# Expert rows in blocks of 256 and of 128 rows, and another order of the work between the attention loop and the second expert layer

## The reference, cut to what matters

```python
xn = layernorm(x)
s = L0_attn(xn)            # 16 heads of 64, ALiBi, two null keys
g = silu(L0_ffn(xn))       # top 1 of 8 experts: gelu(x @ W1[e] + b1[e]) @ W2[e] + b2[e]
x = x + s * g
xn = layernorm(x)
s = L1_attn(xn)            # one head of 128, layer norm, output projection
g = silu(L1_ffn(xn))       # top 2 of 8 experts, capacity C = 2*2*T/8 rows for each
x = x + s * g
```

## Time and profile before

| | |
|---|---|
| median of three runs | 1130.6 us (1126.27 to 1135.07) |
| the profiled execution | 1132.19 us, its span 1130.3 us |
| mean granted TensorE clock | 0.951 |
| busy: TensorE matmul | 1004.9 us, 89% |
| busy: VectorE, ACT, GpSimd | 686.6, 655.2, 673.2 us (about 60% each) |
| DMA | 103.70 MB, mean 92 GB/s |
| chain that ended last | TensorE 62%, VectorE 17%, ACT 7% |

### The profile page before, as it was taken

How to read it: one execution, slowest core, us unless ns; L and a number is a source line. 1 busy time by engine, 2 the same in 40 slices (tenths; PEclk the granted TensorE clock), 3 DMA queues, 4 the chain that set the end, 5 groups by cost and what they waited for, 6 DMA issues and landing times.

```text
span 1130.3 us, 22358 instructions
## 1 busy us (share of the span) xinstructions
PE 1004.9 (89%) x6636; PEld 736.4 (65%) x6636; DVE 686.6 (61%) x2541; ACT 655.2 (58%) x1967; POOL 673.2 (60%) x825
## 2 busy tenths in 40 slices
PE   6688899999999999899999998998889979999940
PEld 2465566666668986566666665666568758989940
DVE  6847776776753346776786777868654443445326
ACT  4329767667754557667666766675554434454534
POOL 5534588888754555676675687887354423545533
PEclk9759899999999999999999999999999889999985
DMA  9200202202526742303302212132130044777755
GB/s 300 58 6 1 43 25 61 65 25 66 160 47 209 221 129 63 74 6 70 65 7 60 54 36 61 34 67 53 40 86 19 29 144 144 214 216 217 214 139 142
DMA packets 97385, 103.70 MB, mean 92 GB/s; under 512 B 10447, under 2 KB 85238, under 8 KB 97040
## 3 DMA queue, kind: packets, MB, share of 16 engines
q1 hardware_dynamic: 90256, 89.96, 30.5%
q0 software_dynamic: 7040, 12.66, 3.3%
HBM read 77.29 MB, written 25.28 MB: 91 GB/s over the span
## 4 chain that ended last, share of the span: by engine, by line
PE 62%; DVE 17%; ACT 7%; issue 6%; POOL 4%; DMA 1%; another core or an unknown queue 1%; SPq 0%; POOLq 0%; DVEq 0%; ACTq 0%
PE bank L1135 11%; PE bank L644 9%; PE bank L633 9%; PE bank L1164 7%; PE bank L1191 5%; PE bank L1179 4%; PE bank L1216 4%; DVE arena L1760 4%; PE bank L1154 3%; ACT arena L1494 3%; DVE arena L1769 2%; POOL arena L910 2%; PE bank L1365 2%; PE bank L1349 1%; ACT arena L1483 1%
## 5 line engine op out<-in xcount | busy, mean ns | idle before, releaser
L1494 ACT ACTIVATE arena<-arena 128x128 f32<-128x128 f32 (+1 forms) x512 | 226.9, 446 | 114.6 <-DVE arena L1760 114.0
L1760 DVE CUSTOM_DVE_ANT_0 arena<-bank,arena 128x128 f32<-128x128 f32 (+1 forms) x512 | 183.0, 413 | 140.8 <-PE bank L1164 133.1
L1135 PE MATMUL bank<-arena 128*128 128x512 f32 x384 | 215.6, 649 | 13.0 <-ACT arena L1483 10.0
L910 POOL TENSOR_TENSOR arena<-arena 128x512 f32<-128x512 f32 x128 | 133.5, 1046 | 146.6 <-ACT arena L1470 141.7
L1769 DVE COPY arena<-bank 128x384 f32<-128x384 f32 x256 | 130.2, 549 | 24.5 <-PE bank L1179 21.4
L607 POOL DMA_INDIRECT expert_out<-arena x78 | 77.0, 988 | 100.8 <-DVE arena L713 85.1
L1470 ACT ACTIVATE arena<-bank 128x512 f32<-128x512 f32 x192 | 112.4, 586 | 31.1 <-PE bank L1135 30.9
L925 POOL TENSOR_TENSOR arena<-arena 128x512 f32<-128x512 f32 x128 | 129.5, 1045 | 1.3
L1164 PE MATMUL bank<-arena 64*128 64x128 f32 (+1 forms) x1024 | 120.8, 355 | 9.6 <-DVE arena L1760 8.9
L1179 PEld LDWEIGHTS bank<-const,arena 128*128 128x128 f32 x768 | 91.9, 142 | 56.8 <-issue 56.6
L1191 PE MATMUL bank<-arena 128*64 128x256 f32 (+1 forms) x1024 | 112.3, 340 | 7.3 <-DVE arena L1769 3.7
(11 more groups left out here) (273 smaller groups left out, 1740.5 us busy)
## 6 DMA issues: line engine op xcount, KB each, us to landing
arena<-in_wp SPq DMA_DIRECT2D x39, 514.0 KB
arena<-recip_rows SPq DMA_DIRECT2D x30, 512.0 KB
XN<-in_wp SPq DMA_DIRECT2D x23, 514.0 KB
arena<-expert_rows SPq DMA_DIRECT2D x62, 129.0 KB
arena<-expert_out SPq DMA_DIRECT2D x16, 256.0 KB, 5.0
arena<-in_b SPq DMA_DIRECT2D x62, 64.0 KB
expert_out<-fill SPq DMA_DIRECT2D x11, 338.6 KB, 8.2
expert_rows<-fill SPq DMA_DIRECT2D x1, 2967.0 KB, 22.0
```

The costliest lines, as they stand in the source:

```text
L910: pool.tensor_tensor(sq[:, i % 2], r, r, ALU.mult).then_inc(S["sq_done"], 1)
L1135: mm = pe.matmul(RING[bnk][:, :], xa[:, p, t * P:(t + 1) * P], wqkv[:, 512 * k:512 * k + 512], start=True, stop=True)
L1494: ins = act.activation(w, w, ACT.Exp, bias=nm[:, p, 16 * t + h:16 * t + h + 1], scale=-1.0, accum_out=den[:, p, 16 * t + h:16 * t + h + 1])
L1760: ins = v.tensor_tensor_reduce(out=SPb[:, c % 2, 384 * k + P * t:384 * k + P * t + n], in0=SBANK[k][:, P * t:P * t + n], in1=alibi[:, h, N ...
```

## The change

**Block sizes.** The unit of an expert's rows becomes 128. The worst case is 39 units in layer 0 and 71 in layer 1. Layer 0 gets `NBIG` = 15 blocks of two units and then 9 of one, layer 1 gets 31 and then 9 (`SMALL`), that is 24 and 40 blocks. Each expert's pairs of units go to the large blocks until these are used up, the units left over to the small ones. A small block has one transpose, half the columns in `up`, half the products in `down`, half the columns on ACT and VectorE, half the row load and one send; its weight loads are whole. Both layers' first rows now come from a table (`rowtab`, also in layer 0). The loops over four cover blocks 4 to 11 at most in layer 0 (`PERIOD`) and 4 to 27 in layer 1; the rest is straight line. Layer 0's tables are made in attention step 1 (`late`), before they were made in step 0.

**Order behind the loop.** Scores have two banks, and TensorE's `step1(b)` ends with the scores of b+2. The last projection uses one bank and stands after steps 0 and 1. The masks of a group are computed before `residual`, and the ranks of group 5 one step earlier. The last norm is earlier on all engines. GpSimd does `scale_out` (L949) before the scatters. SP fills padding rows (128 rows each in place of 256) before the first weights. Also `fold_weights` moves into step 6.

The core of the diff:

```diff
-BLK = 256
+BLK = 128
+DBL = 2 * BLK
...
+UNITS_OF = ((T + E * (BLK - 1)) // BLK, (2 * T + E * (BLK - 1)) // BLK)
+NSMALL = E + 1
+NBIG = tuple((u - NSMALL) // 2 for u in UNITS_OF)
+NBLK0, NBLK1 = (n + NSMALL for n in NBIG)
...
+SMALL = tuple(tuple(range(n, n + NSMALL)) for n in NBIG)
+SMALL_OF_FOUR = ((), ())
+PERIOD = ((4, 11), (4, 27))
...
+        def blocks(v, link, layer, held, nthr):
...
+            link(v.scalar_tensor_tensor(out=cm, in0=held.unsqueeze(2).to_broadcast([P, E, nthr]), scalar=1.0 / BLK,
+                                        in1=cc(C_JJ, nthr).unsqueeze(1).to_broadcast([P, E, nthr]), op0=ALU.mult, op1=ALU.is_gt))
+            link(v.tensor_reduce(half, cm.rearrange("p e (k two) -> p e two k", two=2), AX.X, ALU.add))
+            v.tensor_tensor_scan(FX[:, 1:E + 1], ones[:, 0:E], half[:, :, 1], 0.0, ALU.mult, ALU.add)
+            link(v.tensor_tensor(UNI, half[:, :, 0], half[:, :, 1], ALU.add))
+            v.tensor_scalar(FX[:, 1:E + 1], FX[:, 1:E + 1], float(NBIG[layer]), None, ALU.min)
+            link(v.tensor_tensor_scan(UX[:, 1:E + 1], ones[:, 0:E], UNI, 0.0, ALU.mult, ALU.add))
+            link(v.scalar_tensor_tensor(out=CGX, in0=FX, scalar=-2.0, in1=UX, op0=ALU.mult, op1=ALU.add))
...
+        def owners(v, link, layer):
+
+            FX, _, CGX, _, _, _, _, _, RSJ = TAB[layer]
+            nb, n, cj = of_blocks(layer)
+            v.memset(cj[:, :, 0:1], 1.0)
+            for lo, hi, ends in ((0, nb, FX), (nb, n, CGX)):
+                ins = v.tensor_tensor(cj[:, lo:hi, 1:E + 1], const[0:1, C_JJ:C_JJ + hi - lo].unsqueeze(2).to_broadcast([1, hi - lo, E]),
+                                      ends[0:1, 1:E + 1].unsqueeze(1).to_broadcast([1, hi - lo, E]), ALU.is_ge)
+            link(ins)
+            link(v.tensor_reduce(RSJ[0:1, 0:n], cj, AX.X, ALU.add))
+            v.tensor_scalar(owner[:, 0:n], RSJ[0:1, 0:n], -1.0, float(E - 1), ALU.add, ALU.min).then_inc(S["owner_ready"], 1)
             v.wait_ge(S["owner_ready"], layer + 1)
...
+        def tables(v, link, layer):
...
+            link(v.tensor_tensor(steps[:, :, 0:E], first[:, :, 1:E + 1], first[:, :, 0:E], ALU.subtract))
+            for k, (lo, hi) in enumerate(((0, nb), (nb, n))):
+                ins = v.tensor_tensor(cj[:, lo:hi], cj[:, lo:hi], steps[0:1, k].unsqueeze(1).to_broadcast([1, hi - lo, E + 1]), ALU.mult)
+            link(ins)
+            link(v.tensor_reduce(RSJ[0:1, 0:n], cj, AX.X, ALU.add))
+            for lo, hi, size in ((0, nb, DBL), (nb, n, BLK)):
+                ins = v.scalar_tensor_tensor(out=RSJ[0:1, lo:hi], in0=const[0:1, C_JJ:C_JJ + hi - lo], scalar=float(size),
+                                             in1=RSJ[0:1, lo:hi], op0=ALU.mult, op1=ALU.add)
+            link(ins)
+            v.tensor_scalar(rowtab[layer][:, 0:n], RSJ[0:1, 0:n], float((NOROWS0, NOROWS)[layer]), None, ALU.min)\
+             .then_inc(S["tables_ready"], 1)
...
-            def load_rows(j, q):
-                row = sp.value_load(rowtab[0:1, bass.ds(j, 1)], min_val=0, max_val=NOROWS) if layer else j * BLK
-                src = xe[layer][bass.ds(row, BLK), :].rearrange("(t p) d -> p t d", p=P)
-                sp.dma_start(xb[:, q], src).then_inc(S[f"rows_in{q}"], 16)
-
-            def load_weights(j, q):
-
-                e = sp.value_load(owner[0:1, bass.ds(j, 1)], min_val=0, max_val=E - 1)
+            def load_rows(j, q, i):
+                n = 1 if single(layer, j, q) else 2
+                row = sp.value_load(rowtab[layer][0:1, bass.ds(entry(layer, j, q, i), 1)], min_val=0, max_val=(NOROWS0, NOROWS)[layer])
+                src = xe[layer][bass.ds(row, n * BLK), :].rearrange("(t p) d -> p t d", p=P)
+                sp.dma_start(xb[:, q, 0:n], src).then_inc(S[f"rows_in{q}"], 16)
+
+            def load_weights(j, q, i):
+
+                e = sp.value_load(owner[0:1, bass.ds(entry(layer, j, q, i), 1)], min_val=0, max_val=E - 1)
                 sp.dma_start(wb[:, q], W[bass.ds(e, 1)].rearrange("e p n -> p (e n)")).then_inc(S[f"w_in{q}"], 16)
                 sp.dma_start(b2b[:, q], B2[bass.ds(e, 1)].to_broadcast([P, D])).then_inc(S[f"w_in{q}"], 16)
 
-            def step(j, q):
+            def step(j, q, i):
 
                 sp.wait_ge(S["xT_evac"], j + (base + 1))
-                load_rows(j + NBUF, q)
+                load_rows(j + NBUF, q, i + 1)
                 sp.wait_ge(S["ye_evac"], j + (base + 1))
-                load_weights(j + NBUF, q)
-
-            sp.wait_ge(S["owner_ready"], layer + 1)
+                load_weights(j + NBUF, q, i + 1)
+
             if layer:
-                sp.wait_ge(S["ttr_done"], NB * 16)
-                for j in range(NBUF):
-                    load_weights(j, j)
-                sp.wait_ge(S["tables_ready"], 1)
+                sp.wait_ge(S["pads_ready"], 1)
                 for e in range(E):
                     row = sp.value_load(padtab[0:1, e:e + 1], min_val=0, max_val=NOROWS)
-                    sp.dma_start(xe[1][bass.ds(row, BLK), :].rearrange("(p r) d -> p (r d)", p=P), fill[:, :]).then_inc(S["filled"], 16)
+                    sp.dma_start(xe[1][bass.ds(row, BLK), :], fill[:, 0:ROW]).then_inc(S["filled"], 16)
+                sp.wait_ge(S["ttr_done"], NB * 16)
+                sp.wait_ge(S["owner_ready"], 2)
+                for j in range(NBUF):
+                    load_weights(j, j, 0)
+                sp.wait_ge(S["tables_ready"], 2)
                 sp.wait_ge(S["scattered"], scattered)
                 sp.wait_ge(S["first"], 16 * (NT - 4))
                 sp.wait_ge(S["first3"], 16 * 4)
                 sp.wait_ge(S["filled"], 16 * (1 + NFILL + E))
             else:
+                sp.wait_ge(S["owner_ready"], 1)
                 sp.wait_ge(S["scattered"], scattered)
                 for j in range(NBUF):
-                    load_weights(j, j)
+                    load_weights(j, j, 0)
+                sp.wait_ge(S["tables_ready"], 1)
             for j in range(NBUF):
-                load_rows(j, j)
+                load_rows(j, j, 0)
             if first_rows is not None:
                 first_rows()
-            quads(sp, 0, nblk - NBUF - 1, lambda j, q, i: step(j, q))
+            last = PERIOD[layer][1] - NBUF
+            quads(sp, 0, last, step)
+            for j in range(last + 1, nblk - NBUF):
+                step(j, j % NBUF, j // NBUF)
...
-                for t in range(2):
+                for t in range(1 if single(layer, j, q) else 2):
...
+                n = BLK if single(layer, j, q) else DBL
                 for c in range(FC):
-                    mm = pe.matmul(HB[2 * (q % 2) + c // 2][:, (c % 2) * BLK:(c % 2 + 1) * BLK],
-                                   wb[:, q, c * P:(c + 1) * P], xbT[:, q % 2, :], start=True, stop=True)
+                    mm = pe.matmul(HB[2 * (q % 2) + c // 2][:, (c % 2) * DBL:(c % 2) * DBL + n],
+                                   wb[:, q, c * P:(c + 1) * P], xbT[:, q % 2, 0:n], start=True, stop=True)
...
+                for j in range(NBUF):
+                    gelu(j, j, 0)
+                quads(act, NBUF, PERIOD[1][1], gelu)
+                for j in range(PERIOD[1][1] + 1, nblk):
+                    gelu(j, j % NBUF, j // NBUF)
...
             norm_root(len(SETS) - 2)
+            scale_out(NB - 1, 1)
+            last_ids()
             send_rows(2, 1)
-            last_ids()
-            scale_out(NB - 1, 1)
             send_rows(3, 0)
             for k in range(2):
                 residual0(len(SETS) - 1, k)
             norm_root(len(SETS) - 1)
+            send_rows(3, 1)
             send_rows(4, 0)
-            send_rows(3, 1)
             send_rows(4, 1)
             send_rows(5, 0)
...
+                if b >= 2:
+                    pe.wait_ge(S["ttr1_done"], b - 1)
+                pe.matmul(SC[p][:, 0:P], z1[:, p, 0:P], x[:, 0:P], start=True, stop=True)
+                pe.matmul(SC[p][:, P:P + N], z1[:, p, P:N], x, start=True, stop=True).then_inc(S["s1_full"], 1)
...
-                if b + 1 < NB:
-                    pe.wait_ge(S["ttr1_done"], b + 1)
-                    scores1(b + 1)
...
+                if b + 2 < NB:
+                    scores1(b + 2)
...
+            scores1(1)
             step1(0)
-            ranks1(3, MISC)
+            pe.wait_ge(S["lg_evac"], 1)
+            ranks1(3, RT)
+            for half in range(2):
+                project(NB - 1, 1, 0, half)
             step1(1)
-            pe.wait_ge(S["lg_evac"], 1)
+            for half in range(2):
+                project(NB - 1, 1, 1, half)
+            pe.wait_ge(S["rank_evac"], 5)
             turn_last(9)
-            pe.wait_ge(S["rank_evac"], 5)
-            project(NB - 1, 1, 0, 0)
-            project(NB - 1, 1, 1, 0, Y2)
             step1(2)
             logits_last(9)
-            project(NB - 1, 1, 0, 1)
-            project(NB - 1, 1, 1, 1, Y2)
             step1(3)
             step1(4)
+            pe.wait_ge(S["lg_evac"], 2)
+            turn_last(10)
```

(63 more changed lines are left out.)

216 lines of the change are left out of this document (122 added, 94 removed).

## The result

The changed kernel took 1120.4 us (median of 4 runs, 1114.8 to 1134.5), the kernel before 1131.5 beside it: a ratio of 0.989, 95% interval 0.986 to 0.993. That is 11 to 12 us gained where 25 were predicted, and 1.4 us above the predicted range. Run again in two later groups it had 0.995 (0.991 to 0.998) and 0.991 (0.987 to 0.994).

The account below looks back on a forecast made before the run. TensorE was taken to bound the expert stages and attention loop, with waits and low clock in the stretch between. Savings of 14.6 + 1.7 - 1.0 + 10.0 = 25.3 us gave a median of 1105 us, 8 in 10 between 1094 and 1119.

Parts of the forecast that it names:

- What bounds a small block: Expert stages: SP's issues bound small blocks at 2.77 us each; nine take 22.5 us, saving 7.3 us per layer, 14.6 in both.
- this is below SP's 2.77: Small blocks: buffer's way back takes 4.7 and 5.2 us for two blocks, 2.3 and 2.6 us each, under SP's limit.
- The landing of the weights: Small blocks: weights and b2 land 3.0 to 5.5 us after issue, 4.0 taken; upper costs 1.5 us per layer, lower gains 1.0.
- 8 x 3.73 = 29.8 us: Expert stages: TensorE time of the eight large blocks in a layer, set against nine small ones at 17.0 without waits.
- The end: After the last `add_b2`: one send per block ends 2.5 us after it instead of 4.2, 1.7 us saved.
- Layer 0's tables: Attention step 1 and `blocks`: some 10 more short VectorE instructions, 2 to 2.5 us, of which 1.0 us lost.
- The stretch between: Between attention loop and layer 1's experts: mask waits, low clock and bank waits go, 10 us saved, between 0 and 20.
- The rival by which the stretch gives nothing: Behind the attention loop: each wait removed shows up as another, for GpSimd or reciprocals; 1115 us, chance 0.18.
- the piece that the prediction left "where it is": Stretch between loop and layer 1's experts: a 5.71 us piece of the chain that no engine caused, assumed unchanged.
- The sum: Whole kernel: 14.6 + 1.7 - 1.0 + 10.0 = 25.3 us saved, median becomes 1105 us.
- The clock: Small blocks: TensorE's clock falls to 1.2 GHz, nine take 34 us, 11.7 more per layer; 1128 us, chance 0.07.
- one of the prediction's own signs of being wrong: Small blocks: a TensorE clock below 0.9 in them was named as showing the prediction wrong.

Follow-up runs that it names:

- run 1: The changed kernel, unedited, once more for an undisturbed profile: 1119.1 us, 0.995 of the kernel before.
- run 10: The changed kernel, unedited, on the same chip as the kernel before in its group: 0.991 of the kernel before.
- run 8: The changed kernel with small blocks' weight loads cut from 514 KB to 32 KB: nine small blocks took 4.0 and 2.3 us less than the changed kernel's mean.
- Run 3: The changed kernel with the old order behind the loop, small blocks kept: 0.999 of the kernel before, 1.2 us less.
- run 9: The kernel before, unedited, once more for its profile: 1112.0 us in its group.
- run 11: The kernel before with only the order behind the loop changed, again, on another chip: 0.991 of the kernel before.
- run 6: The changed kernel with small blocks' row and expert numbers loaded into SP's registers before the layer: the nine small blocks took no less time.
- run 2: The kernel before with only the order behind the loop changed, all blocks at 256 rows: 0.995 of the kernel before, 5.7 us less.
- runs 1, 2, 4 and 13 to 18: Besides the first two: small blocks spread (0.996), then variants of send wait, registers, weight bytes, spreading and tables; the kernel before needs 1126 to 1131 us there.
- runs 5 to 12: Kernel before, changed kernel, order alone, and edits to small blocks' row numbers, SP registers or weight bytes; the kernel before needs 1112 to 1114 us there.
- run 17: The changed kernel with own columns for row numbers, numbers in registers, and layer 0's tables divided over four pairs: 0.984 of the kernel before.

## Why the prediction was wrong

*What bounds a small block: wrong, and this is the largest miss.* The step that failed is "this is below SP's 2.77", the way back of a small block. It took the second send (1.29 us) out of the sum of the earlier trace rows. That counts a single send as landing sooner by as much. In that row 1057.37, the start of the first send, to 1061.93, its buffer's next `evac_x`, is 4.56 us; a small block's single send took 4.41 in run 1 and 4.1 on average in run 10. It starts about half a microsecond from the weight load of 514 KB that the same `add_b2` releases. Run 8 shows the bytes of that load to be a part of the delay; the rest stays open. So the way back stayed 6.3 us, a small block took 2.8 to 3.1 us on average, and nine took 28.0 and 25.4 (means of runs 1, 3, 10) instead of 22.5. Against 28.3 and 28.4 for eight large ones (means of before and runs 9, 11) that is 0.2 and 3.0 saved, **3.2 us, not 14.6**. The last five small `up` of layer 1 stand 2.3 to 3.1 us apart in run 1, near the predicted 2.8. SP's queue is full in a part of that stretch, with 2.75 us from one weight load to the next:

```profile
1062.60 0.34 SPq L638 DMA_DIRECT2D arena<-in_wp  x1
...
1064.23 0.34 SPq L633 DMA_DIRECT2D arena<-expert_rows  x1
...
1065.35 0.34 SPq L638 DMA_DIRECT2D arena<-in_wp  x1
```

The two intervals before are 3.7 and 3.0 us, so SP and the way back are close together as limits; run 6 shows that SP alone isn't the one to lift. In layer 0 `tanh` and `silu2` lengthen the way, and its small `up` stand 2.0 to 5.5 apart. The landing of the weights, where the prediction put its range, held `up` for 1.2 us at most (for b2, run 1, layer 0).

Two more steps of the same term were wrong. It set 8 x 3.73 = 29.8 us against a count that begins at the end of the last large `down`. From there only seven `up`, eight `down` and six pairs of transposes follow, 28.1 and 28.2 us in the profile of before: 3 us of the 14.6 were never there. And nine small blocks are 17.8 us of TensorE's work at full clock, not 17.0.

*The end: right.* The last `add_b2` to the end of the last send is 1073.05 to 1075.18, 2.1 us, against 4.2; predicted 2.5. From the last `down` to the end of the program the profiles went from 42.9 to 40.0 (run 1), in run 10 only from 41.9 to 41.5.

*Layer 0's tables: wrong, 4.6 us and not 1.0.* The step that failed was to size them as "some 10 short instructions, 2 to 2.5 us". They were 7.0 us, some of them over 1 us for a few elements, and they stood in one piece between two `rows_max` for which TensorE had no work in store.

*The stretch between: right, where nothing else happened.* `ranks1` of groups 4 and 5 starts without a wait, the low clock is gone in run 11 (though not in run 10), and runs 9 and 11 give 10.3 us (7.6 with the loop); the time of run 11 gives 10. The rival by which the stretch gives nothing falls with that. On the chips with the unknown piece the same edit gave 5.7 us (run 2): the piece that the prediction left "where it is" grew from 5.7 to 11.0 us.

*The sum.* -3.2 - 2.1 + 4.6 - 7.6 = -8.3 us on a chip without the unknown piece; run 10 measured -10 (6 to 14 by its interval), and its profile is 7.9 shorter than run 9's. So the sum agrees with the runs, within intervals of 4 us, once the two steps are put right: 14.6 + 1.7 - 1.0 for the blocks was 15.3, and is 3.2 + 2.1 - 4.6 = 0.7. Run 3 measured 1.2.

*The clock* as a rival came true in part. Nine small blocks never took the 34 us that it named, but the clock fell below 0.9 in them in some profiles, one of the prediction's own signs of being wrong. After a wait of 5 us in run 10's layer 0 the next 4 us have 0.62 of the full clock:

```profile
394.00:398.00 4.00, 4.00 (x24) 4.00 (x24) 0.68 (x5) 1.80 (x7) 1.02 (x2) 0.62 0.62 176
```

Set against 17.8 us of work at full clock, TensorE's work in the nine blocks is on average 1.7 us longer in layer 0 and 1.4 in layer 1 in runs 1, 3 and 10: an estimate of 3 us of what was missing. The waits weigh more: in run 1 layer 0's small blocks have 1.00 throughout and take 27.2 all the same, with TensorE idle for 9.4 us of it.

## What to carry to other kernels

Halving a block's work halves nothing that is issued or loaded whole: before counting the saved matmuls, walk the whole loop from a buffer's result to its next use and ask of each transfer what lands ahead of it. A transfer's landing is to be taken from a row with the same neighbours: beside loads a send landed here up to 3.2 us later than alone. A wait for it belongs where the buffer is written again (here `add_b2`), not where a number of four bytes is copied. When eight blocks become nine, count both from the same instant. Where one busy engine feeds another, small arithmetic is paid by the piece: the same instructions held TensorE for 4.1 us as one piece and not at all as four.

## What the runs showed of the hardware

- A send of 64 KB by GpSimd landed 2.1 us after its start when no loads were beside it, and 2.6 to 5.3 us after it beside loads of 514 KB (runs 6 and 10); with these cut to 32 KB it still took 2.4 to 4.2 (run 8).
- The same kernel's nine small blocks had a granted TensorE clock of 1.00 in one profile (run 1, layer 0) and 0.88 in another (run 10), with TensorE's work at 17.8 and 20.7 us.
- Behind the attention loop, five issues of SP took 12.06 us and VectorE stood for 11.12 us, while GpSimd scattered rows (run 2); pieces of this kind stand in the profiles of before and of runs 1, 2, 4 and 13 to 18, and in none of runs 5 to 12, taken on two other chips, where the kernel before took 12 to 18 us less in all. Its cause wasn't settled.
- Two instructions on 135 elements of one partition took 2.54 us in run 10. The same two, one pair of the step later, took 0.93 us in run 17.

```profile
137.44 0.93 DVE L484 TENSOR_TENSOR arena<-arena 1x135 f32<-1x135 f32 x2
```
